# Part of the next image's first layer moved from the experts' phase into the attention phase, and the rest of it six chunks earlier

## What is computed

```
x  = x + spiking_attention(group_norm(x))            # 32 groups; spike(v) = round(clip(v, 0, 4)) / 4
     xs = spike(group_norm(x))
     q, k, v = spike(bn(W_q xs)), spike(bn(W_k xs)), spike(bn(W_v xs))
     a = spike(q (k^T v) * scale * 2)   per head of 24; out = bn(W_p a)
t  = tokens(x)
t  = t + softmax attention(layer_norm(t))            # 6 heads of 32, causal, 1024 x 1024 scores
t  = t + mixture of 4 experts(layer_norm(t))         # top 2 by a softmax gate; 192 -> 768 -> 192, exact gelu
```

## Time and profile before

| | us |
|---|---|
| median of 3 runs (1701.23 to 1702.93) | 1701.42 |
| the profiled execution, its own time | 1703.11 |
| its span, from the first to the last instruction | 1701.1 |
| PE busy, share of the span | 1590.3, 93% |
| DVE busy | 1188.9, 70% |
| ACT busy | 904.1, 53% |
| POOL busy | 173.3, 10% |
| granted clock of TensorE, mean share of 2.4 GHz | 0.976 |

### The profile page before, as it was taken

How to read it: one execution, slowest core, us unless ns; L and a number is a source line. 1 busy time by engine, 2 the same in 40 slices (tenths; PEclk the granted TensorE clock), 3 DMA queues, 4 the chain that set the end, 5 groups by cost and what they waited for, 6 DMA issues and landing times.

```text
span 1701.1 us, 32601 instructions
## 1 busy us (share of the span) xinstructions
PE 1590.3 (93%) x13148; PEld 1028.3 (60%) x13148; DVE 1188.9 (70%) x2537; ACT 904.1 (53%) x1329; POOL 173.3 (10%) x247
## 2 busy tenths in 40 slices
PE   3689999999999999899998999999999999999998
PEld 1424676546665567656765567655766557665666
DVE  6685775767767676867759578576776777686643
ACT  3206654466545665456553665446654566535654
POOL 2210102001110003000120010200121000300100
PEclk9759999999999999999999999999999999999999
DMA  4112002010111002010020100201011100200000
GB/s 158 52 29 63 1 1 66 8 41 2 26 41 48 1 1 66 2 48 1 2 66 1 48 2 1 66 13 36 2 38 30 48 2 1 66 1 11 1 11 10
DMA packets 25129, 47.27 MB, mean 28 GB/s; under 512 B 7410, under 2 KB 16946, under 8 KB 23700
## 3 DMA queue, kind: packets, MB, share of 16 engines
q1 hardware_dynamic: 15728, 27.85, 5.9%
q0 software_dynamic: 6144, 9.45, 2.4%
q10 hardware_dynamic: 3108, 7.91, 1.3%
HBM read 19.82 MB, written 6.29 MB: 15 GB/s over the span
## 4 chain that ended last, share of the span: by engine, by line
PE 67%; DVE 23%; ACT 4%; issue 3%; POOL 1%; DMA 1%; SPq 0%; DVEq 0%; ACTq 0%; POOLq 0%
PE ps L437 20%; PE ps L708 16%; PE ps L655 10%; DVE mx L1148 7%; PE ps L472 6%; PE ps L596 3%; DVE acc L1314 3%; DVE room L1330 3%; PE ps L516 2%; DVE norm_stats L989 2%; PE ps L444 1%; PE ps L503 1%; ACT room L874 1%; PE ps L476 1%; DVE gn_st L1031 1%
## 5 line engine op out<-in xcount | busy, mean ns | idle before, releaser
L874 ACT ACTIVATE room<-ps,b_sb 128x512 f32<-128x512 f32 x384 | 263.2, 685 | 459.8 <-PE ps L437 459.8
L708 PE MATMUL ps<-wout_h,room 128*128 128x192 f16 x3072 | 459.4, 246 | 5.4 <-DVE acc L1314 5.4
L1330 DVE SCALAR_TENSOR_TENSOR room<-room 128x512 f16<-128x512 f32 x384 | 262.7, 687 | 179.2 <-ACT room L882 174.2
L708 PE MATMUL ps<-wout_l,room 128*128 128x192 f16 x1536 | 377.9, 246 | 0.0
L708 PEld LDWEIGHTS ps<-wout_h,room 128*128 128x128 f16 x3072 | 286.5, 98 | 45.7 <-DVE acc L1314 11.8
L854 ACT ACTIVATE room<-ps 128x1024 f32<-128x1024 f32 (+3 forms) x288 | 224.8, 811 | 161.0 <-PE ps L476 123.6
L1148 DVE TENSOR_REDUCE mx<-ps 128x2 f32<-128x1024 f32 (+3 forms) x288 | 265.8, 952 | 36.3 <-PE ps L600 19.2
L882 ACT ACTIVATE room<-room 128x512 f16<-128x512 f32 x384 | 241.9, 630 | 33.8 <-ACT room L874 0.4
L655 PE MATMUL ps<-room,v 128*64 128x512 f32 (+3 forms) x1152 | 232.9, 488 | 0.9 <-DVE o L1280 0.9
L596 PE MATMUL ps<-qk 96*128 96x512 f16 (+3 forms) x576 | 159.8, 349 | 38.7 <-DVE mx L1148 30.3
L708 PEld LDWEIGHTS ps<-wout_l,room 128*128 128x128 f16 x1536 | 150.4, 98 | 27.3
(11 more groups left out here) (201 smaller groups left out, 2291.0 us busy)
## 6 DMA issues: line engine op xcount, KB each, us to landing
xc<-x_ch SPq DMA_DIRECT2D x8, 768.0 KB, 5.7
qk<-qk_all SPq DMA_DIRECT2D x96, 64.0 KB, 2.4
qk<-qk_all POOLq DMA_DIRECT2D x96, 64.0 KB, 2.6
out<-acc ACTq DMA_DIRECT2D x16, 384.0 KB, 2.4
xt<-x_tok SPq DMA_DIRECT2D x7, 768.0 KB, 7.0
qk<-qk_all POOLq DMA_DIRECT2D x96, 32.0 KB, 2.0
qk<-qk_all SPq DMA_DIRECT2D x96, 32.0 KB, 2.3
room<-w_in SPq DMA_DIRECT2D x2, 1024.0 KB, 8.5
```

The costliest lines, as they stand in the source:

```text
L708: mm = pe.matmul(dst, hid[:, s, tok], w[:, n, :], start=(k == 0 and m == 0 and t % 2 == 0), stop=False, skip_group_check=True)
L874: act.activation(h32[:, i % N_H, :], ps[:, H_BANK[i], :], ACT.Gelu, scale=1 / (U_SCALE * W_SCALE), bias=b1_sb[:, n:n + 1])\
L1330: V.scalar_tensor_tensor(out=h_l[:, s, :], in0=h32[:, s, :], scalar=A_SCALE, in1=h_h[:, s, :], op0=ALU.mult, op1=ALU.subtract)\
```

## The change

The front is cut into two generators. `early` holds the group norm and the spikes of the input (`xs`), and for the images 1 to 7 it is woven into the attention phase of the image before, by the table `EARLY_AT` in units of score blocks. `front` holds the rest, for images 1 to 7 by a new `FRONT_AT` that begins with q at chunk 4; for image 0 all due times stay what they were (`FIRST_AT`). The group sums use bank 2 instead of 7, and for that the attention's Wo product waits for the variance. q uses the banks 6 and 7 for both token halves, k and v use banks 6 and 7 (two instead of four), k^T v bank 6. From q (k^T v) on, everything stands 5.5 chunks earlier (18.5 becomes 13), the maxima 6 chunks earlier (28.5) and with 2 a chunk instead of 2.75. The channel layout of an image is loaded one image further ahead. POOL's power for the group norm stands ahead of that of the tail.

```diff
+FIRST_AT = {"stats": 3, "sums": 4.5, "sums2": 5.5, "variance": 5.5, "clip": 6, "relu": 7.5, "xs": 8.5,
+            "q": 10.5, "q1": 12.5, "q_int": 11.5, "kv": 12.5, "kv_int": 13, "kvm": 16.5, "kvm_split": 17.5,
...
+EARLY_AT = {"stats": 0, "sums": 3, "sums2": 4.5, "variance": 4.5, "clip": 7, "relu": 8, "xs": 9.5}
+FRONT_AT = {"q": 4, "q1": 6, "q_int": 5, "kv": 7, "kv_int": 7.5, "kvm": 11, "kvm_split": 12,
+            "attn": 13, "attn_int": 13, "p": 14, "residual": 14, "norm": 16.5, "turn": 18.5,
+            "high": 19.5, "low": 19.5, "qk": 20.5, "qk_lo": 20.5, "v": 24.5, "maxima": 28.5}
-PER_CHUNK = 2.75
+PER_CHUNK = 2
+KVM_BANK = 6
+def group_bank(img):
+    return 2 if img else 7
+def query_bank(later, b, m):
+    return 6 + m if later else 6 - 2 * b + m
+def key_value_bank(later, t):
+    return 6 + t % 2 if later else 4 + (t + 2) % 4
...
@@ SP
             load_later(0)
+            load_channels(1)
             for img in range(B - 1):
                 spread(img)
                 if img == 0:
                     load_later(1)
-                load(img + 1)
+                load_tokens(img + 1)
+                if img + 2 < B:
+                    load_channels(img + 2)
...
 # PE
+            def early(img, when):
+                yield when["sums"]
+                pe.wait_ge(gn_rhs, at(gn_rhs, img, 1))
+                if img > 1:
+                    pe.wait_ge(y_used, at(y_used, img - 1, 0))
+                pe.matmul(ps[0:CC, group_bank(img), 0:2], group, gn_s[:, :], start=True, stop=True)\
+                  .then_inc(gn_ps, 1)
+                yield when["sums2"]
+                pe.wait_ge(gn_rhs, at(gn_rhs, img, 2))
+                pe.matmul(ps[0:CC, group_bank(img), 2:4], group, gn_v[:, :], start=True, stop=True)\
+                  .then_inc(gn_ps, 1)
...
                 for b in range(NB):
-                    yield FRONT_AT["q"] + 2 * b
+                    yield when["q1" if b else "q"]
                     if b == 0:
                         pe.wait_ge(xs_ready, at(xs_ready, img, 2))
+                        if later:
+                            pe.wait_ge(e_done, at(e_done, img, 0))
                     elif later:
-                        pe.wait_ge(gate_used, at(gate_used, img, 0))
+                        pe.wait_ge(q_relu, at(q_relu, img, 2))
...
-                    if t < 4:
+                    if later:
+                        pe.wait_ge(*((q_relu, at(q_relu, img, t + 3)) if t < 2 else
+                                     (kv_relu, at(kv_relu, img, t - 1))))
+                    elif t < 4:
                         pe.wait_ge(q_relu, at(q_relu, img, t + 1))
...
 @@ PE, tail of token half 0
+                elif img + 1 < B:
+                    pe.wait_ge(var_ready, at(var_ready, img + 1, 1))
...
 @@ PE and ACT, attend
                 aside = Aside(tail(img, 0, later))
+                following = Aside(early(img + 1, EARLY_AT) if img + 1 < B else iter(()))
...
+                    following.until(j)
                     aside.until(j)
...
 @@ ACT
+            def early(img, when):
+                yield when["relu"]
                 act.wait_ge(gn_ready, at(gn_ready, img, 1))
-                if later:
-                    act.wait_ge(o_done, at(o_done, img, 0))
+                if img:
+                    act.wait_ge(a_int, at(a_int, img, 0))
                 for c in range(2):
-                    yield FRONT_AT["xs"] - 1 + c
+                    yield when["relu"] + c
                     act.activation(tx[:, c, :], xc[:, c, :], ACT.Relu, scale=g_rstd[:, c:c + 1],
                                    bias=gn_b[:, c:c + 1]).then_inc(x_relu, 1)
...
 @@ POOL, attend
+                if img + 1 < B:
+                    group_power(img + 1)
                 power_of_tail(0)
...
 # DVE: early holds the statistics ("stats"), the mean ("sums"), the variance ("variance"), the Newton
 # step ("clip") and the spikes ("xs", "xs" + 1), with the same instructions as before
```

More of the change, by code:

```diff
@@ L730, in experts @@
                 following.finish()
-            first = Aside(front(0, False))
+            first = Aside(chain(early(0, FIRST_AT), front(0, False)))
             pe.wait_ge(small_in, 16 * n_small)
-            first.until(FRONT_AT["sums"])
+            first.until(FIRST_AT["sums"])
             pe.wait_ge(bn_ready, 2)
@@ L1022, in normalized_block, with spike, early @@
                  .then_inc(signal, 1)
-            def front(img, later):
-                steps = Count()
-                yield FRONT_AT["stats"]
+            tx = tmp[0:CC, 0:2 * N].rearrange("p (c n) -> p c n", c=2)
+            def spike(img, steps, dst, t, signal):
+                V.tensor_scalar(t, t, 4.0, MAGIC, ALU.min, ALU.add).then_inc(front_step, 1)
+                dve.wait_ge(front_step, at(front_step, img, steps.more(1)))
+                V.tensor_scalar(dst, t, MAGIC, None, ALU.subtract).then_inc(signal, 1)
+            def early(img, when, steps):
+                yield when["stats"]
                 dve.wait_ge(x_ch_in, at(x_ch_in, img, 16))
@@ L1284, in attend @@
                 aside = Aside(tail(img, 0, later))
+                following = Aside(early(img + 1, EARLY_AT, steps) if img + 1 < B else iter(()))
                 ends = run_ends()
@@ L1349, in newton @@
                 step(V.scalar_tensor_tensor(out=into, in0=a, scalar=1.5, in1=y, op0=ALU.add, op1=ALU.mult))
-            first = Aside(front(0, False))
+            steps = Count()
+            first = Aside(chain(early(0, FIRST_AT, steps), front(0, False, steps)))
             dve.wait_ge(rows_in, 16 * n_rows)
             step(V.tensor_scalar(bn_t[:, 0, :], bn_st[:, :, 3], 1e-5, None, ALU.add))
-            first.until(FRONT_AT["stats"])
+            first.until(FIRST_AT["stats"])
             dve.wait_ge(setup_act, 1)
@@ L1392, in _ @@
                 first.until(PIECE_AT[n])
-            first.until(FRONT_AT["maxima"] - 0.5)
+            first.until(FIRST_AT["maxima"] - 0.5)
             dve.wait_ge(late_in, 16 * n_late)
@@ L1399, in _ @@
             first.finish()
-            attend(0, False)
+            steps = Count()
+            attend(0, False, steps)
             for img in range(B - 1):
-                experts(img, Aside(front(img + 1, True)))
-                attend(img + 1, True)
+                experts(img, Aside(front(img + 1, True, steps)))
+                steps = Count()
+                attend(img + 1, True, steps)
             experts(B - 1, Aside(iter(())))
```

132 lines of the change are left out of this document (63 added, 69 removed).

## The result

The changed kernel takes 1774.47 us (median of four runs, 1771.96 to 1776.57), the kernel before took 1702.18 us beside it: a ratio of 1.0419, with a 95% interval of 1.0403 to 1.0435. It is slower by 72 us, where 62 were forecast, and inside the range of 1731 to 1784. The profiled execution has a span of 1773.7 us and a mean granted clock of 0.955 (0.976 before).

A forecast was written before the change was run, and what follows sets the result against it. PE's sequential work was taken as the bound, plus its waits: 14.6 us an image against 7.4, +50 us, and 12 for the clock, 62 over 1703.1; median 1763 us, range 1731 to 1784.

The forecast's parts named there:

- maxima: PE's waits for DVE's maxima stay only where an expert is added, chunks 32, 38, 44: 3.9 us an image instead of 6.1.
- p of half 1: New PE wait at chunk 15: DVE's rounding of half 1 queues behind the gate's comparisons; 3.4 us lost an image.
- transpose: PE waits as the norm's statistics stand behind chunk 16's low half: 2.5 us lost an image instead of 0.7.
- first projection of the second layer: At chunk 20 DVE's low half waits for ACT, so PE waits: 0.7 us lost an image, nothing before.
- attention, group sums: At block 3 PE waits for DVE's group statistics, begun after the last expert's addition: 1.6 us lost an image.
- attention, blocks 7 to 14: Newton step and spikes delay run 1's normalization: 2.5 us lost an image, 1.5 us from Exps delayed by Relus inside it.
- clock: PE's idle time at p's wait halves the granted clock once an image: 1.7 us lost, 12 us in all.
- rival of a phase that absorbs the early part: Idle DVE and ACT in the attention phase take the early part for nothing: 1735 us, chance 0.12.
- rival of a clock that holds: No clock falls after the new waits on PE: +50 us, 1751 us, chance 0.18.
- worse rival: ACT loads a table around each Relu between Exps, 5.1 us an image: 1799 us, chance 0.06.
- faster rival: Gate's comparisons not ahead of half 1's rounding at chunk 15, so the maxima's relief remains: about 1670 us, chance 0.10.
- SP and POOL: SP standing at the spikes until block 11 and POOL at the group variance until block 5 cost nothing.

The follow-up runs named there:

- kernel 1: The changed kernel with the gate's comparisons due at chunk 22 instead of 13: 1726.57 us.
- kernel 2: The changed kernel with unused matmuls of 512 columns on PE, 15 ahead of p's wait and 10 ahead of the first transpose: 1745.33 us.
- kernel 5: kernel 1 with the layer norm's statistics at the start of chunk 16's list on DVE instead of its end: 1709.87 us.
- kernel 9: The changed kernel with q (k^T v) of half 1 and its rounding due at 13.5 instead of 14, ahead of the expert's addition: 1732.29 us.
- kernel 11: The changed kernel with the maxima leaving out the due times 33, 39 and 45: 1746.48 us.
- kernel 3: The changed kernel with only its early part in the attention phase; front from k and v on at old due times, 2.75 maxima a chunk: 1734.68 us.
- kernel 6: kernel 1 with the two spikes on DVE at block 24 of the attention phase instead of 9.5: 1726.38 us.
- kernel 7: kernel 1 with the first group sums at block 5 and all that follows them from block 16 on, spikes at 24: 1703.05 us.
- kernel 8: kernel 1 plus the edits of kernel 5, kernel 7 and kernel 11, and both halves' q (k^T v) and rounding ahead of the addition: 1660.52 us.
- kernel 10: kernel 8 with the maxima from chunk 27 instead of 28.5: 1649.36 us, ratio 0.9682 to the kernel before.
- kernel 4: The kernel before with only the maxima changed, from chunk 31.5 instead of 34.5 and 2.25 a chunk instead of 2.75: 1685.36 us.

## Why the prediction was right in sign and mechanism, and low by 10 us

Lost per image, each with 0.16 us a wait added as in the prediction:

| term | forecast | measured |
|---|---|---|
| maxima | 3.9 | 4.0 |
| p of half 1 | 3.4 | 3.4 |
| transpose | 2.5 | 2.2 |
| first projection of the second layer | 0.7 | 0 (0.6 with a full clock, kernels 1 and 2) |
| attention, group sums | 1.6 | 1.6 |
| attention, blocks 7 to 14 | 2.5 | 2.3 |
| k and v over two banks | 0 | 0 |
| sum | 14.6 | 13.4 |
| clock | 1.7 | 4.8 |

With the 7.4 us that the kernel before loses, the measured terms give 13.4 + 4.8 - 7.4 = 10.8 an image, where the period grew by 10.3.

- *The waits in the experts' phase* came out within 0.3 us, those for p and the maxima within 0.1. Counting both engines' lists from a common start, with durations from the rows, was enough; kernels 1, 5 and 9 cut or removed the waits for p and the transpose one by one by moving just the pieces of DVE's list that the working had named.
- *The clock was the mis-sized term.* The prediction took "one fall each, as long as that of 3.4 us". There were two, the one after p twice as long: 3.2 + 1.6 us instead of 1.7, and 3.1 x 7 = 22 us more. The end of two falls (24 us) was named, with both taken as 3.4 us; 4.8 x 7 = 34 us lies above it. Kernel 2 shows this price with the waits in place, kernel 1 that p's fall goes with p's wait. Kernel 11 bears the sizes out image by image: with the same waits, the matmuls behind p run through 3.2 us sooner in its image without a fall than in the changed kernel, and 1.5 us sooner in those with a fall of 3.4 us. The smaller sum of waits (13.4 for 14.6, 8 us in seven images) took part of it back, and so did 0.5 us an image that the two sums leave open.
- *The rule of the Trainium skill*, "TensorE: Matmul & The Clock Gate", section "Why this matters for your kernels" (no gaps above about 3 us), fits p's wait of 3.2 us in the changed kernel. It does not bound the cost here: the clock also fell after the transpose's 2.1 us, and in kernels 3 and 6 after waits of 1.4 and 1.5 us, and it held after 3.2 us in one image of kernel 11.
- *First projection.* The 0.7 us was right for a full clock. In the changed kernel PE came too late to wait.
- *One reading of the rows* was off: the period of 201.3 us recurs six times, not seven. The first, with the fall at 320.1 us in it, takes 203.0 us, so that fall cost 1.7 us, the price that the prediction took. Its one image stood for the others all the same.
- *Attention, blocks 7 to 14.* The size was right and its composition wrong: the waits for Exps (1.3 with the 0.16 each) and the one for `o` (1.0) stand one behind the other. I had put 2.5 on `o` alone, with the Exps' 1.5 inside it; PE, held up twice by the Exps, came later to `o` by that much. Kernel 6 took only the second away and won 1.1.
- *The rival of a phase that absorbs the early part* was false as the change placed it (4.4 us), and nearly true as kernel 7 placed it (0.6 us). The idle time of the earlier trace rows was there; it was not at blocks 3 and 7 to 14.
- *The rival of a clock that holds* was false: all fourteen waits at p and at the transpose were followed by a fall.
- *The worse rival* fell: Relu runs between Exps with no table load. The Trainium skill, "ScalarE: Activation LUTs", section "Table sets: the hidden batching unit", has relu in every set, and the trace agrees: two loads an image.
- *The faster rival* named the right condition, the comparisons out of the rounding's way. Kernel 1 makes it so and is still slower, for the attention phase and the transpose keep their waits. With those removed too (kernels 8 and 10) the relief of the maxima comes out, and more: 54 us under before.
- *SP and POOL* added nothing: behind the first image no wait of PE ends with a load or a power. POOL's power stays in the chain ahead of the transpose, where DVE waits 1.7 us for it (1.5 before).

Left open: what decides that one wait is followed by a fall and another of the same length is not. In the changed kernel every image repeats the one before at the same distance, and falls in the same place; in kernel 11, whose waits for p and the transpose are the same, the falls differ by image.

## What to carry to other kernels

In lists written out by hand, a block that moves by 5.5 steps against other work that recurs every six meets it at a new place: lay both engines' lists side by side over one period before moving it. Work moved into an idle phase costs by where it stands: the same group norm and spikes cost 4.4 us an image in front of a result that PE wanted and 0.6 us with all but the statistics and the first group sums at blocks 16 to 25. And a wait of a few us on PE is to be priced with the clock behind it; here two falls cost 4.8 us on top of 5.6 us of waits.

## What the runs showed of the hardware

- Behind the first 200 us the granted clock was 0.50 for stretches of 3.4 or 6.8 us and 1.00 otherwise; one of 3.4 us costs 1.6 us where PE is the bound, one of 6.8 us 3.2.
- It fell after waits far shorter than the 3.2 us that I had thought of, but not after each of them. Waits of PE behind the first 200 us of the profiled executions, and how many were followed by a fall:

| idle of PE, place | followed by a fall |
|---|---|
| 3.2 us, p | changed kernel 7 of 7, kernel 11 6 of 7 |
| 2.7 us, transpose | kernel 9 4 of 7 |
| 2.1 us, transpose | changed kernel 7 of 7, kernel 1 0 of 7, kernels 6 and 7 3 of 7 each, kernel 11 4 of 7 |
| 1.5 or 1.6 us, a maximum | kernel before 1 of 7, kernel 3 4 of 7, kernel 4 0 of 7 |
| 1.4 us, group sums | changed kernel and kernel 1 0 of 6, kernels 2 and 5 1 of 6, kernels 3, 6 and 9 2 of 6, kernel 11 3 of 6 |
| 1.3 us, maxima, two an image | changed kernel and kernels 1, 2, 5, 6, 7 and 9 0 of 14 each |

The shortest two that were followed, in the timeline of kernel 3's PE, with falls at 528.7 and 549.2 us:

```profile
527.82 0.34 PE L631 MATMUL ps<-qk 96*128 96x384 f16 x1 [1.49 <-DVE mx L1199]
...
548.59 0.33 PE L513 MATMUL ps<-gn_s,kst 96*96 96x2 f32 x2 [1.38 <-DVE gn_s L1090]
```

- Feeding PE 25 matmuls of 512 columns with unused products kept the clock full and made the kernel 29 us faster than it was with the same waits left empty (1745.3 against 1774.5).
- A slow clock can hide a later wait: the first projection's 0.6 us was gone in the changed kernel and back in kernels 1 and 2. In kernel 11 it was gone in two images, whose fall began 0.6 us or more after the transpose did, and there in the five others.
